# A six-layer decoder kernel: input normalised by halves, keys projected once and laid out by DMA, self-attention's output by halves

## The reference

```python
x = x + _L0_attn_ref(_layernorm(x), ...)       # gated linear attention, 16 heads of 8, causal sums
x = x + _L0_xattn_ref(_layernorm(x), ctx, ctx, lengths, ...)
x = x + _L0_ffn_ref(_layernorm(x), ...)        # 8 experts, top 2, two loops
x = x + _L1_attn_ref(_layernorm(x), ...)       # selective scan, 16 states
x = x + _L1_xattn_ref(_layernorm(x), ctx, ctx, bias, padding, ...)
x = x + _L1_ffn_ref(_layernorm(x), ...)        # quantised, 512 hidden
```

## Time and profile before

| | us |
|---|---|
| median of 3 runs (lowest, highest) | 657.33 (656.75, 658.64) |
| the profiled execution, its own time | 661.11 |
| its span, first to last instruction | 659.4 |
| mean granted TensorE clock | 0.881 of full speed |
| busy: TensorE, VectorE, ScalarE, GpSimd | 533.6, 455.0, 264.9, 139.1 |

### The profile page before, as it was taken

How to read it: one execution, slowest core, us unless ns; L and a number is a source line. 1 busy time by engine, 2 the same in 40 slices (tenths; PEclk the granted TensorE clock), 3 DMA queues, 4 the chain that set the end, 5 groups by cost and what they waited for, 6 DMA issues and landing times.

```text
span 659.4 us, 8927 instructions
## 1 busy us (share of the span) xinstructions
PE 533.6 (81%) x3166; PEld 305.2 (46%) x3170; DVE 455.0 (69%) x1177; ACT 264.9 (40%) x452; POOL 139.1 (21%) x102
## 2 busy tenths in 40 slices
PE   4888589999969999999999853655564899999633
PEld 3344366666526666666666510122121555555312
DVE  6379845777265536766646458999996458889785
ACT  3532025555534314324324225555530244444642
POOL 6226000000000000030000005899992100000010
PEclk9789778999988889999999975678887799999955
DMA  4000070000010000000000000000001000000000
GB/s 121 0 4 1 0 224 1 2 1 2 1 40 1 0 0 1 1 0 5 1 0 1 0 1 0 0 0 0 1 0 40 0 1 2 1 3 1 1 4 29
DMA packets 10095, 8.20 MB, mean 12 GB/s; under 512 B 1634, under 2 KB 9124, under 8 KB 10052
## 3 DMA queue, kind: packets, MB, share of 16 engines
q1 hardware_dynamic: 10052, 7.64, 4.1%
HBM read 6.98 MB, written 0.52 MB: 11 GB/s over the span
## 4 chain that ended last, share of the span: by engine, by line
PE 62%; DVE 28%; ACT 4%; issue 3%; POOL 2%; DMA 1%; SPq 0%; DVEq 0%; ACTq 0%; POOLq 0%
PE PS L1064 17%; PE PS L1075 9%; PE PS L681 8%; DVE VA L1515 6%; DVE PS L1502 5%; PE PS L743 4%; PE PS L668 3%; DVE PS L1508 3%; PE PS L728 3%; PE PS L719 2%; PE PS L436 2%; PE PS L700 2%; PE PS L753 1%; PE PS L340 1%; DVE SCR L923 1%
## 5 line engine op out<-in xcount | busy, mean ns | idle before, releaser
L1064 PE MATMUL PS<-XNT,KSA 128*128 128x512 f32 x256 | 122.5, 616 | 2.8 <-DVE E L1269 2.0
L878 ACT ACTIVATE E<-PS 128x512 f32<-128x512 f32 x128 | 71.2, 596 | 68.7 <-PE PS L728 42.9
L1269 DVE TENSOR_TENSOR E<-E,PS 128x512 f32<-128x512 f32 x64 | 43.9, 687 | 61.2 <-ACT E L1122 60.8
L1122 ACT ACTIVATE E<-PS 128x512 f32<-128x512 f32 x64 | 38.1, 597 | 111.4 <-PE PS L1064 109.0
L728 PE MATMUL PS<-QM,KP 32*128 32x256 f32 x512 | 82.0, 403 | 0.8 <-ACT E L878 0.8
L681 PE MATMUL PS<-KP,QP 32*128 32x256 f32 x512 | 79.8, 407 | 1.7 <-DVE MXT L923 0.9
L1075 PEld LDWEIGHTS PS<-KSA,E 128*128 128x128 f32 x512 | 64.3, 197 | 18.0 <-issue 17.0
L1064 PEld LDWEIGHTS PS<-XNT,KSA 128*128 128x128 f32 x256 | 46.2, 194 | 46.3 <-issue 42.3
L1075 PE MATMUL PS<-KSA,E 128*128 128x128 f32 x512 | 64.1, 280 | 1.3 <-DVE XN L1260 1.3
L681 PEld LDWEIGHTS PS<-KP,QP 32*128 32x128 f32 x512 | 52.3, 187 | 22.4 <-issue 10.2
L923 DVE CUSTOM_DVE_ANT_0 SCR<-PS,KSA 128x256 f32<-128x256 f32 x128 | 46.5, 420 | 23.3 <-PE PS L681 22.2
(11 more groups left out here) (269 smaller groups left out, 824.8 us busy)
## 6 DMA issues: line engine op xcount, KB each, us to landing
KSA<-in_w SPq DMA_DIRECT2D x2, 1024.0 KB, 7.0
X<-in_x SPq DMA_DIRECT2D x1, 512.0 KB, 4.3
SCR<-in_ctxT SPq DMA_DIRECT2D x1, 512.0 KB, 5.8
SCR<-in_fside SPq DMA_DIRECT2D x1, 512.0 KB, 4.6
out_x<-X SPq DMA_DIRECT2D x8, 64.0 KB, 1.5
wx<-in_w_x SPq DMA_DIRECT2D x1, 384.0 KB, 6.6
wself<-in_w_self SPq DMA_DIRECT2D x1, 256.0 KB, 7.2
KSA<-in_w1T SPq DMA_DIRECT2D x1, 256.0 KB, 10.5
```

What stands on the lines that cost most here:

```text
L878: act.activation(slot(m, j), weight_bank(m, j), ACT.Exp).then_inc(sig("exps"), 1)
L1064: ins = pe.matmul(bank(2 * (g % 3) + o), w[:, e, c * P:(c + 1) * P], XNT[:, tokens_of(p)], start=True, stop=True)
L1122: act.activation(E6[:, 4 + g % 2, :], bank(2 * (g % 3)), ACT.Silu).then_inc(sig("silu"), 1)
L1269: dve.tensor_tensor(E6[:, g % 4, :], E6[:, 4 + g % 2, :], bank(2 * (g % 3) + 1), ALU.mult)\
```

## The change

- x is loaded in two halves, first in the queue, and the weights of self-attention right behind. The first normalisation uses the `entry_` helpers by halves (entry 0), so the layers' entries are now 0, 1 and 2. The bias rows come from two reductions.
- Keys: one projection of the unpadded weights per layer (`keys_project`), one compact copy (`keys_take`), and 16 DMAs that move each head's 8 rows into its band (`keys_spread`). ScalarE fills KP beforehand in layer 0 (`keys_clear`). WP keeps only the query weights. A key bias comes from a new small load, `bkey`.
- ScalarE sorts the weights by head. GpSimd clears VX first, and multiplies CTM only when XN is done.
- Features of sequences 0 and 1 use different banks. The gate of sequence 1 is done after the first weighed sum.
- Self-attention's output goes by halves of four tiles: half 0 in tiles 4 and 5, with its residual, statistics and the norm of entry 1 half 0 ahead of the last sum; half 1 inside the first round of cross-attention, where the values of layer 0 are now projected too.
- Queries of sequence 1 stand behind the first scores, in both layers.

```diff
+        ENTRY_XN = (0, 1, 5)
+        ENTRY_BANK = ((2, 3), (6, 4), (3, 4))
...
+            if e == 0:
+                dve.wait_ge(sig(("x_first", "x_second")[half]), 16)
...
-                ins = pe.matmul(bank(first_bank + half), WP[:, L, 1, g, :], (CTM if L == 0 else CT)[:, t],
+                ins = pe.matmul(bank(first_bank + half), wx[:, L, 1, :], (CTM if L == 0 else CT)[:, t],
                                 start=True, stop=True)
...
+        def keys_take(act, L, first_bank):
+            act.wait_ge(sig("keys_psum"), L + 1)
+            if L == 0:
+                ins = act.activation(COMPACT[L], two(first_bank), ACT.Copy)
+            else:
+                act.wait_ge(sig("bkey_in"), 16)
+                ins = act.activation(COMPACT[L], two(first_bank), ACT.Identity, bias=bkey[:, 1:2])
+            ins.then_inc(sig("keys"), 1)
+
+        def keys_clear(act, bands):
+
+            act.wait_ge(sig("row_bias"), 1)
+            for g in bands:
+                act.activation(KP[:, g, :], rowbias[:, 0, 1, 0:1].to_broadcast([P, T]), ACT.Copy)\
+                    .then_inc(sig("keys_clear"), 1)
...
+        def keys_spread(sp, L):
+
+            sp.wait_ge(sig("keys"), L + 1)
+            if L == 0:
+                sp.wait_ge(sig("keys_clear"), NG)
+            for h in range(H):
+                g, i = divmod(h, HG)
+                sp.dma_start(KP[32 * i:32 * i + DH, g, :], COMPACT[L][h::H, :]).then_inc(sig("key_rows"), 16)
...
             pool.wait_ge(sig("ctx_in"), 16)
+            pool.wait_ge(sig("xn"), 2)
             pool.tensor_tensor(CTM, CT, VMASK, ALU.mult).then_inc(sig("ctx_masked"), 1)
...
+        FEATURE_BANK = (6, 4, 6, 6)
...
             features(0)
-            keys_project(pe, 0, 2, 0)
+            context_keys(pe)
             features(1)
-            pe.wait_ge(sig("vx_ready"), 1)
-            keys_project(pe, 0, 3, 2)
             for j in range(NT):
                 cumulate_outer(j)
                 if j % QT == 1 and j // QT + 2 < B:
                     features(j // QT + 2)
-                if j >= 5:
-                    project_mixed(j - 5)
-                if j >= 4:
-                    turn_mixed(j - 4)
-            project_mixed(B - 1)
+                if j == 4:
+                    turn_mixed(pe, 0)
+                if j == 5:
+                    project_mixed(pe, 0)
...
             feature(0)
-            feature(1)
+            feature_soft(1)
             for j in range(NT):
                 b, q = divmod(j, QT)
                 weigh_sum(j)
+                if j == 0:
+                    feature_gate(1)
                 if q == 1:
                     divide(b)
                     if b + 2 < B:
                         feature(b + 2)
-                if j >= 5:
-                    add(j - 5)
+                if j == 5:
+                    self_residual(dve, 0)
+                    entry_variance(dve, ch, 1, 0)
                 if j == 6:
-                    entry_variance(dve, ch, 0, 0)
-            entry_norm(dve, ch, 0, 0)
-            key_bias(dve)
-            add(B - 1)
+                    entry_norm(dve, ch, 1, 0)
...
             queries(0)
-            queries(1)
             pe.wait_ge(sig("neg_rows"), 16 * HG * (L + 1))
-            pe.wait_ge(sig("vx_const"), 2)
-            pe.wait_ge(sig("vx_ready"), L + 1)
+            pe.wait_ge(sig("key_rows"), 16 * H * (L + 1))
             pe.wait_ge(sig("const_late"), 1)
             if L == 1:
                 pe.wait_ge(sig("bias_parts"), 1)
+            else:
+                turn_mixed(pe, 1)
             for i in range(HG):
                 scores(0, i)
+            if L == 0:
+                project_mixed(pe, 1)
+                context_values(pe)
+            queries(1)
...
                 if k == 0:
-                    entry_norm(dve, ch, L, 1)
+                    if L == 0:
+                        self_residual(dve, 1)
+                        entry_variance(dve, ch, 1, 1)
+                        key_bias(dve)
+                    entry_norm(dve, ch, L + 1, 1)
...
-            load(X[:, :, :], inp["x"].rearrange("(j p) d -> p j d", p=P), "x_in")
+            tokens = inp["x"].rearrange("(j p) d -> p j d", p=P)
+            load(X[:, 0:4, :], tokens[:, 0:4, :], "x_first")
+            load(X[:, 4:8, :], tokens[:, 4:8, :], "x_second")
+            load(wself[:, :, :], inp["w_self"].rearrange("w p d -> p w d"), "wself_in")
```

364 lines of the change are left out of this document (166 added, 198 removed).

## The result

The changed kernel took **638.8 us** (median of four runs, 636.84 to 639.8) beside 657.38 for the kernel before: ratio 0.9713, 95% interval 0.9688 to 0.9738. Measured again later (run e0), six runs gave 635.29 beside 656.58: ratio 0.9669 (0.9635 to 0.9702). The forecast was 636.0. By the medians the gain is 18.6 the first time and 21.3 the second, where 21.4 was forecast. The profiled execution took 639.32 with a span of 637.6, against 661.11 and 659.4: 21.8 less.

What follows compares the result with a forecast made beforehand. TensorE held 62% and VectorE 28% of the chain, but the stretches to be changed were bound by engines waiting in turn. Gains of 11.9 + 2.3 + 6.1 + 1.1 = 21.4 off the 657.33 median gave 636.0 us, range 630 to 643.

Steps and rivals of the forecast that it cites:

- Part 1: Start to first weighed sum: X in halves, transposes first and one key projection bring it to 25 from 38.70.
- So products release it now: Start of cumulation 0: GpSimd's products at 22.6, not the key copy at 20.8 to 21.9, come last.
- likeliest case: Whole kernel: the sum of all parts holds, 21.4 gained, 636.0 us; chance 0.55.
- rival (a): TensorE's clock stays low through the start and again through the entry, giving back about 5: 641 us; chance 0.18.
- the forecast's own sign: Division 0 ending after 38, other distances kept, would show part 1 wrong, by clock or landing of X.
- Part 3: Division of sequence 0 to division of sequence 3: 29.6 instead of 32.0, ending at 64.4, 2.3 gained.
- Part 2: First weighed sum to division of sequence 0, with the moved gate costing 3: ends 34.8 against 46.66, 11.9 gained.
- Part 4: Division of sequence 3 to the second half's queries at 76.4: 11.9 against 18.06, 6.1 gained.
- rival (b): Bridge gets no shorter: values in ScalarE's and TensorE's queues delay second norm and queries 1; 642 us; chance 0.12.
- rival (c): Everything catches the full clock and X lands at 3.5: some 5 more gained, 631 us; chance 0.09.
- Part 5: Tail of cross-attention 0: three of four key projections go, one of them unhidden, 1.1 gained.
- Rival (d): The 20 small key DMAs don't stream, 5.98 each in SyncE's queue, scores wait 74: 710 us; chance 0.03.

Runs made afterwards that it cites:

- e0: The changed kernel itself, unedited, measured and profiled again: 635.29 us beside 656.58 for the kernel before, ratio 0.9669.
- first trace: Profile of one execution of the changed kernel from its first measurement: 639.32 us, span 637.6.
- second trace: Profile of one execution of the same changed kernel, taken in e0: span 636.0 us.
- e2: Changed kernel with GpSimd's two clearings of VX moved from the front of its queue to behind the masked context: 636.14 us, ratio 0.9685.
- e9: Changed kernel with GpSimd's clearing of VX behind the masked context and cut in four pieces: 637.63 us, ratio 0.9709.
- e8: Changed kernel with VX cleared in four pieces behind the masked context, plus 22 and 5 unused TensorE products around the first transposes: 636.59 us, ratio 0.968.
- e7: Changed kernel with the gate of sequence 1 put ahead of the first weighed sum again: 641.5 us, ratio 0.9749.
- e6: Changed kernel with residual, statistics and norm of the next entry's half 0 moved from VectorE's loop to behind the last division: 643.39 us, ratio 0.9791.
- e11: Changed kernel with the values' projection and its copies moved from behind the first scores to behind the last cumulation: 640.08 us, ratio 0.9736.
- e4: Changed kernel with layer 1's queries of sequence 1 put ahead of the first scores again: 637.93 us, ratio 0.971.
- e5: Changed kernel with each of the 16 key-layout transfers cut in 8, 128 issues in both layers: 675.42 us, ratio 1.0278.
- e1: Changed kernel with the key projection moved from between features 0 and 1 to behind cumulation 0: 641.23 us, ratio 0.9752.
- e3: Changed kernel with 36 unused identity products on TensorE ahead of its first transposes and 10 between the two transpose groups: 638.84 us, ratio 0.9713.

## Why the prediction held, and which of its steps did not

**Part 1 was right about the chain and missed the length of the low clock.** Forecast 25, traces 25.83 and 29.10. The four steps before are close: first half of X landed at 3.97 at the latest (4.4), features began at 13.16 and 13.69 (12.3; XN's second half took 2.12 and 1.86 beside GpSimd instead of 1.11, and the transposes of half 1 had to wait for it). The sum took the features at 4.5, near the low level, and let the clock rise behind them. In the first trace features 0, the projection and half of features 1 had the low level: 5.29, 3.78, and 1.91 for the next product. The step that fell there is "So products release it now": features 1 released cumulation 0. In the second trace each duration came out within 1 of the forecast, from a start 1.4 late. So the likeliest case and the first half of rival (a) both occur in one kernel; e0 shows it. By the forecast's own sign, division 0 ended after 38 (38.29), the first trace says that part 1 was wrong, and it was the clock; the second, at 34.81, says that it was right. Rival (a) put 3.0 on the start (projection 1.7, features 1.3); measured it is 3.3 at the first weighed sum, 2.7 at queries 3 and 1.6 at the end of the span. Its other 1.9 did not come: the values ran at the full level, 1.95 in the first trace.

A second thing was missing from part 1: the clearing of VX at the front of GpSimd's queue. The forecast moved it there only as a gain for part 3. It holds VectorE's four tiny copies to 4.61, and so ScalarE's first work and the root, by about 1 us (6.58 against 5.40, 5.46 and 5.56 in e2, e9 and e8). XN then starts only 0.2 to 0.5 earlier without it, since VectorE does the second half's statistics first, and the price at the first weighed sum is not told from the scatter of the start.

**Part 2.** From the first sum to the end of division 0: 9.8 forecast, 9.19 and 8.98 measured, mostly because the gate took 2.5 and 2.3 instead of 3. The Trainium skill's exclusive lock (SBUF — State Buffer, section "SBUF: two separate sides") was read by the forecast as making all three operations pay a product, an estimate of 3.6. In the traces one of three paid in full (0.82, 1.18, 0.42; and 0.61, 1.18, 0.42), in e7 all three (3.7). The third got through in 0.42 where it began after GpSimd's four products had ended (33.94, after 33.62, in the first trace), so these rows agree with the lock: which operations pay depends on where they fall against the products. The memset's 1.92 is gone as forecast (the same step takes 0.18 at 55.8).

**Part 3.** 29.6 forecast for the stretch to division 3; 29.34 and 29.42 measured. The wait for TensorE before sum 5, forecast at 0.5, was 0.42.

**Part 4.** 12.0 forecast from division 3 to queries 2 (the text's 11.9 is 12.0 by its own marks), 12.46 and 13.13 measured: 5.6 and 4.9 gained instead of 6.1. Queries 0 took 3.59 and 3.78 instead of 3.35. The step from maxima to queries 2 took 8.97 where 8.5 was forecast: VectorE's own maxima, residual, statistics and norm are one chain, and the root waited for its variance by 0.63, not for the values. e6 confirms the mechanism (5.3 lost without the early half), e11 removes rival (b).

**Left at nothing, but a gain.** Queries 2 met the full clock (1.99 instead of 3.78), and so did the scores behind them: queries 2 to queries 3 took 4.97 instead of 7.71, **2.7 gained**.

```profile
80.09 1.99 PE L678 MATMUL PS<-XNT,WP 128*128 128x256 f32 x8 [0.69 <-ACT XNT L275]
```

Before, TensorE worked 3.9 of the 5.7 us ahead of queries 2; now queries 1 and eight scores run there, and it works 5.1 of 5.7. That this is the reason is argued for layer 0; e4 tests it in layer 1 only. The forecast put queries 2 in 1.99 into rival (c).

**Part 5.** 1.1 forecast, 0.9 measured. **Layer 1's order**, "nothing (bounds +0.5 and −0.5)": measured 1.0 gained, outside the bounds. The working looked at what both wait for, the copy of queries 0, and not at what runs just before queries 2; e4 shows that with the order put back queries 2 are at the low level again.

**Transfers.** 20 issues in 12.2 us, ended at 35.6 (34 forecast). Rival (d)'s mechanism, issues one after the other, is real, and e5 paid for it in full; its price, 5.98 each, isn't: an issue took 0.61.

**The sum.** Forecast 21.4. First trace: 8.4 + 2.7 + 5.6 + 2.7 (clock) + 0.9 + 1.0, and 0.5 over the experts: 21.8. Second: 11.9 + 2.6 + 4.9 + 2.7 + 0.9 + 1.0, and 0.7 lost over the experts: 23.3 (the spans: 23.4). In the first trace parts 1 and 2 fell 3.5 short (8.4 for 11.9) and the unforecast clock gains in the entries gave 3.7 back. That the total fits is therefore partly luck. The forecast also took the gain off the median of the kernel before, although the marks come from an execution 3.8 above it; whether that execution's extra time lies in stretches that the change shortens is unknown, and the medians alone give 18.6 and 21.3.

What stays open: what decides in one execution when the clock rises after the features begin, from 2.3 us after (e0) over 11 (first trace) to more than 15 (e1). And the experts' stretch, from the last residual of cross-attention 0 to the first scan, varied between 219.6 (e1) and 223.9 (e11) among kernels that don't differ there, which no edit here explains.

## What to carry to other kernels

Work that stands in a queue ahead of a long chain is worth more than its own duration: replacing four padded projections and copies by one, with the layout left to transfers under cover, gave 7 of 9.6 us at the first weighed sum. When one norm's output feeds the next stage, do its first half inside the tail of the last loop; the loop pays the same work, and the bridge gets 5 us shorter. When costing a reordering on TensorE, ask for each burst what ran just before it: moving one batch of queries behind the first scores was worth 1 us in layer 1 although it waited for the same thing.

## What the runs showed of the hardware that was not expected

- One kernel, two executions: 512-column feature products at 1.9 to 2.1 until 24.3 in the one, until 16.0 in the other, from nearly the same start (13.16, 13.69); in e1 the low level lasted from 13.12 to past 28.5 with TensorE nearly always busy. Work from 1.57 on brings the full level to the first transposes (0.60 instead of 1.09). Behind 1.61 of idle time in e3 and 1.60 in e8 cumulation 0 was at the low level in whole or in part (3.78, 2.88), while behind 1.37 in e0 and 1.20 in e2 it was at the full one (1.99, 1.98). Whether the length of the gap decides isn't shown.
- The profile's table by windows shows a granted clock of 1.00 for 13 to 24 in the first trace although those products ran at half speed. At the start of these spans durations tell the level, that column doesn't.
- VectorE's copy of three elements began at 1.94 beside GpSimd's clearing (1.47 to 4.02) and ended at 4.61: so it was held through that, the next (to 4.27) and a third (to 4.59), not for one instruction only; with the two clearings of VX moved away (e2) it took 0.17. Statistics of X at 3.97 took their usual 0.87 beside the same clearings. GpSimd's queue at that point:

```profile
1.47 2.55 POOL L1864 MEMSET VX<- 128x2944 f32 x1
3.96 0.31 POOL L1865 MEMSET VX<- 128x128 f32 x1
4.12 0.47 POOL L1866 MEMSET masks<- 128x384 f32 x1
```

- An issue in SyncE's queue costs 0.61 us for 32 KB and for 4 KB alike.
